# A selective scan with 16 states a channel: products with C taken four groups at a time, and loads of decays moved forward in the queue

## The reference, cut to what matters

```
u, z = split(h @ in_proj_w);  u = silu(conv(u))
dt_r, Bm, Cm = split(u @ x_proj_w);  dt = softplus(dt_r @ dt_proj_w + dt_proj_b)
A = -exp(A_log)
for t in range(512):
    hst = exp(dt[t] * A) * hst + dt[t] * B[t] * u[t]     # 256 x 16 states
    y[t] = sum over the 16 states of hst * C[t]
y = (y + u * D) * silu(z);  return y @ out_proj_w
```

## Time and profile before

| | us |
|---|---|
| median of 3 runs | 1230.9 (1224.32 to 1238.44) |
| profiled execution | 1228.28 |
| its span, first to last instruction | 1226.5 |
| VectorE busy in the span | 938.6 (77%) |
| TensorE busy | 871.2 (71%) |
| GpSimd busy | 701.0 (57%) |
| ScalarE busy | 505.5 (41%) |
| first product with B of batch 1, last of batch 8 | 482.3, 1202.4 |

### The profile page before, as it was taken

The page is one execution under the profiler, slowest core; times in us unless marked ns, Lnnn a source line. Parts: engine busy times, 40 slices in busy tenths (PEclk is TensorE's granted clock), DMA queues, the critical chain, the costliest instruction groups (busy, mean ns, idle before and its releaser), DMA issues. The chain is left out here.

```text
span 1226.5 us, 12808 instructions
## 1 busy us (share of the span) xinstructions
PE 871.2 (71%) x3620; PEld 412.1 (34%) x3620; DVE 938.6 (77%) x1280; ACT 505.5 (41%) x840; POOL 701.0 (57%) x427
## 2 busy tenths in 40 slices
PE   3668988888888656676587687688777688664552
PEld 0123333333333323344244344344434344311120
DVE  3467787977977445799469879688979779899973
ACT  0112212123123322473376386385495485663230
POOL 1021122031113561379569877569989879789996
PEclk9568788788897867699689899797999889875575
DMA  4886746666450352767766766767877767646631
GB/s 127 208 180 144 187 140 153 184 171 152 118 142 14 99 155 63 155 145 165 185 196 176 188 207 167 158 215 172 207 217 169 182 207 174 206 141 126 163 86 28
DMA packets 102849, 192.30 MB, mean 157 GB/s; under 512 B 13147, under 2 KB 68124, under 8 KB 90364
## 3 DMA queue, kind: packets, MB, share of 16 engines
q1 hardware_dynamic: 91516, 183.07, 57.2%
q0 software_dynamic: 11264, 8.43, 4.2%
HBM read 146.80 MB, written 32.06 MB: 146 GB/s over the span
## 5 line engine op out<-in xcount | busy, mean ns | idle before, releaser
L1681 POOL TENSOR_TENSOR hs<-hs,c_rep 128x1024 f32<-128x1024 f32 x128 | 332.0, 2604 | 87.7 <-DVE hs L1931 86.9
L1922 DVE TENSOR_TENSOR p_s_du<-p_s_du,b_rep 128x512 f32<-128x512 f32 x256 | 175.4, 685 | 49.5 <-PE p_s_du L2029 46.2
L2029 PE MATMUL p_s_du<-block_in,spread 96*128 96x512 bf16 x256 | 112.9, 442 | 115.5 <-DVE hs L1931 109.0
L1931 DVE TENSOR_TENSOR_SCAN hs<-decays,p_s_du 128x512 f32<-128x512 f32 x132 | 161.1, 1221 | 13.5 <-DVE p_s_du L1922 0.5
L1931 DVE TENSOR_TENSOR_SCAN hs<-slots,p_s_du 128x512 f32<-128x512 f32 x100 | 122.1, 1221 | 19.7 <-ACT slots L1826 9.7
L802 DVE TENSOR_TENSOR value_prod<-p_eb_y_acc,v 128x512 f32<-128x512 f32 x128 | 83.9, 685 | 56.6 <-PE p_eb_y_acc L1109 47.1
L513 POOL TENSOR_TENSOR sc<-ex,ex_part 128x1024 f32<-128x1024 f32 x8 | 17.0, 2129 | 171.6 <-ACT ex_part L619 171.6
L1826 ACT ACTIVATE decays<-decays,a_neg 128x512 f32<-128x512 f32 x132 | 91.7, 718 | 49.4 <-DMA decays<-dt_rows 39.3
L1720 POOL DMA_INDIRECT y_xr<-moe_sums,position x64 | 105.4, 1647 | 10.8 <-issue 8.2
L1686 POOL TENSOR_TENSOR y_hid<-y_hid,g_in 128x512 f32<-128x512 f32 x64 | 99.0, 1548 | 20.3 <-DVE y_hid L1944 19.8
L2029 PEld LDWEIGHTS p_s_du<-block_in,spread 96*128 96x128 bf16 x256 | 26.1, 102 | 249.4 <-DVE hs L1931 179.0
(11 more groups left out here) (193 smaller groups left out, 1751.6 us busy)
## 6 DMA issues: line engine op xcount, KB each, us to landing
decays<-dt_rows SPq DMA_DIRECT2D x33, 1024.0 KB
qb<-rq_rows SPq DMA_DIRECT2D x32, 1024.0 KB, 13.5
slots<-dt_rows SPq DMA_DIRECT2D x25, 1024.0 KB
wm<-in_wmoe SPq DMA_DIRECT2D x48, 384.0 KB
moe_rows<-zeros SPq DMA_DIRECT2D x8, 774.0 KB, 6.0
xg<-moe_rows SPq DMA_DIRECT2D x48, 129.0 KB
stack<-ex_part SPq DMA_DIRECT2D x96, 64.0 KB
block_in<-y_part SPq DMA_DIRECT2D x192, 32.0 KB
```

What stands on the lines that cost most here:

```text
L1681: nc.gpsimd.tensor_tensor(hs[:, n:n + 2], hs[:, n:n + 2], c_rep[p][:].unsqueeze(1).to_broadcast([128, 2, T]), ALU.mult)\
L1922: nc.vector.tensor_tensor(p_du[:, k % 2], p_du[:, k % 2], b_rep[p][:], ALU.mult).then_inc(dbu_done.sem, 1)
L1931: nc.vector.tensor_tensor_scan(hs[:, n % NA], home(8 * (b - 1) + k // 4)[:, bass.ts(j, T)], p_du[:, k % 2], 0.0, ALU.mult, ALU.add).then_i ...
L2029: nc.tensor.matmul(p_du[:, k % 2], spread[:, i], block_in[:, (2 * b + s) % NB, j], start=True, stop=True).then_inc(du_full.sem, 1)
```

## The change

- `times_c` takes four groups an instruction and waits for all four scans; it is called at k = 4, 8, ... 28 and at k = 0 of the next batch, where it was called at every even k. `gather_y` waits for one such instruction instead of two. On GpSimd the experts' `hidden` and `steps` come ahead of it within a k.
- `load_decays` comes first among a group's issues, ahead of weights and rows, and at other k: 0, 4, 8, 12, 16 for quads 3 to 7 (before: 2, 6, ... 18), and 22, 24, 28 for quads 0 to 2 of the next batch (before: 22, 26, 30). Weights come ahead of rows.
- Later: the skip of the second half by one group (4 to 5), its gate (5 to 6), its projection (9 to 13), the result (11 to 15), silu (5 to 6), the copies of B and C (16 to 19), the stores of the tiles by two groups.
- Earlier by one group: `log_in`, `softplus_cut`, `softplus_end`, `steps`.

```diff
--- before.py
+++ after.py
@@ -1400,7 +1400,7 @@
     da_done = count("da_done", GROUPS)
     dbu_done = count("dbu_done", GROUPS)
     scanned = count("scanned", GROUPS)
-    hc_done = count("hc_done", GROUPS // 2)
+    hc_done = count("hc_done", GROUPS // 4)
     gathered = count("gathered", GROUPS // 4)
     y1_done = count("y1_done", ST)
     y_done = count("y_done", ST)
@@ -1443,7 +1443,7 @@
                     plan.append((dict(rows=begin_at - 8 + 2 * h, weights=begin_at - 6 + 2 * h, turn=begin_at + h, gate=begin_at + 2 + h,
                                       hidden=then + 2 if h else begin_at + 6, up=then if h else begin_at + 4,
                                       half=then + 1 if h else begin_at + 5, down=then + 5 if h else then + 1,
-                                      weigh=then + 6 if h else then + 2, store=then + 8 if h else then + 4),
+                                      weigh=then + 6 if h else then + 2, store=then + 10 if h else then + 6),
                                  b, h, tile, len(plan) + 1))
     tile_unit = {tile: v for _, _, _, tile, v in plan if tile is not None}
 
@@ -1608,20 +1608,20 @@
                     tail(k)
                     if k == 23:
                         load_xr(0)
+                if b == 1 and k in (4, 8, 12, 15, 18):
+                    load_decays(1, {4: 3, 8: 4, 12: 5, 15: 6, 18: 7}[k])
+                if 1 < b <= B and k % 4 == 0 and k < 20:
+                    load_decays(b, (k + 12) // 4)
+                if nxt and k in (22, 24, 28):
+                    load_decays(b + 1, (k - 20) // 4)
+                for _, _, j, _ in due(b, k, "weights"):
+                    if j is not None:
+                        load_weights(j)
                 for _, _, j, _ in due(b, k, "rows"):
                     if j is not None:
                         load_rows(j)
-                for _, _, j, _ in due(b, k, "weights"):
-                    if j is not None:
-                        load_weights(j)
-                if b == 1 and k in (4, 8, 12, 15, 18):
-                    load_decays(1, {4: 3, 8: 4, 12: 5, 15: 6, 18: 7}[k])
-                if 1 < b <= B and k % 4 == 2 and k < 20:
-                    load_decays(b, (k + 10) // 4)
                 if b == 4 and k == 30:
                     load_xr(1)
-                if nxt and k % 4 == 2 and k > 20:
-                    load_decays(b + 1, (k - 22) // 4)
                 for _, _, j, _ in due(b, k, "store"):
                     if j is not None:
                         store_tile(j)
@@ -1633,7 +1633,7 @@
                 if nxt:
                     if k == 10:
                         store_bc(b + 1)
-                    if k == 16:
+                    if k == 19:
                         repeat_bc(b + 1, 1 - p)
                     if k in (19, 21):
                         store_dt(b + 1, (k - 19) // 2)
@@ -1674,11 +1674,11 @@
 
         def times_c(b, p, i):
 
-            pool.wait_ge(scanned.sem, scanned.at(b, 2 * i + 2))
+            pool.wait_ge(scanned.sem, scanned.at(b, 4 * i + 4))
             if i == 0:
                 pool.wait_ge(bc_in.sem, bc_in.at(b))
-            n = (GROUPS * (b - 1) + 2 * i) % NA
-            nc.gpsimd.tensor_tensor(hs[:, n:n + 2], hs[:, n:n + 2], c_rep[p][:].unsqueeze(1).to_broadcast([128, 2, T]), ALU.mult)\
+            n = (GROUPS * (b - 1) + 4 * i) % NA
+            nc.gpsimd.tensor_tensor(hs[:, n:n + 4], hs[:, n:n + 4], c_rep[p][:].unsqueeze(1).to_broadcast([128, 4, T]), ALU.mult)\
                 .then_inc(hc_done.sem, 1)
 
         def hidden(v):
@@ -1729,18 +1729,18 @@
                 turn = GROUPS * (b - 1) + k - 14
                 if 0 <= turn < 4 * GT and turn % 2 == 0:
                     send(*divmod(turn // 2, GT))
-                if old and k == 0:
-                    times_c(b - 1, q, GROUPS // 2 - 1)
-                if new and k and k % 2 == 0:
-                    times_c(b, p, k // 2 - 1)
+                if nxt and k in (17, 19):
+                    steps(b + 1, q, (k - 17) // 2)
                 for _, _, j, v in due(b, k, "hidden"):
                     hidden(v)
-                if old and k == 5:
+                if old and k == 0:
+                    times_c(b - 1, q, GROUPS // 4 - 1)
+                if new and k and k % 4 == 0:
+                    times_c(b, p, k // 4 - 1)
+                if old and k == 6:
                     gate_y(b - 1, q, 1)
                 if new and k == 21:
                     gate_y(b, p, 0)
-                if nxt and k in (18, 20):
-                    steps(b + 1, q, (k - 18) // 2)
                 if (b, k) in bring:
                     fetch(*bring[b, k])
 
@@ -1869,7 +1869,7 @@
                         gated(b + 2, (k - 26) // 3)
                 if not nxt:
                     continue
-                if k == 5:
+                if k == 6:
                     silu_u(b + 1, q)
                     silu_z(b + 1, q)
                 if k == 9:
@@ -1880,7 +1880,6 @@
                     exp_z(b + 1)
                 if k == 14:
                     one_more(b + 1)
-                if k == 15:
                     log_in(b + 1)
                 if k in (20, 23):
                     first_part(b + 1, (k - 20) // 3)
@@ -1962,17 +1961,17 @@
                     tail(k)
                 for _, _, j, v in due(b, k, "half"):
                     half(v)
-                if old and k == 4:
+                if old and k == 5:
                     skip(b - 1, q, 1)
-                if old and k == 11:
+                if old and k == (15 if nxt else 11):
                     result(b - 1)
                 if new and k == 20:
                     skip(b, p, 0)
                 if not nxt:
                     continue
+                if k == 15:
+                    softplus_cut(b + 1)
                 if k == 16:
-                    softplus_cut(b + 1)
-                if k == 17:
                     softplus_end(b + 1)
                 if k in (21, 24):
                     second_rest(b + 1, (k - 21) // 3)
@@ -2030,7 +2029,7 @@
 
         def gather_y(b, q):
 
-            pe.wait_ge(hc_done.sem, hc_done.at(b, 2 * q + 2))
+            pe.wait_ge(hc_done.sem, hc_done.at(b, q + 1))
             if q % 4 == 0:
                 pe.wait_ge(y1_done.sem, y1_done.at(b, q // 4) if q else y1_done.at(b - 1))
             for k in range(4 * q, 4 * q + 4):
@@ -2132,7 +2131,7 @@
                         gather_y(b, (k - 7) // 4)
                 if old and k == 3:
                     gather_y(b - 1, GROUPS // 4 - 1)
-                if old and k == 9:
+                if old and k == (13 if nxt else 9):
                     out_proj(b - 1, 1)
                 if new and k == 24:
                     out_proj(b, 0)
```

## The result

| | before | after |
|---|---|---|
| median on the same chip, 4 runs each | 1232.87 us | 1269.54 us (1266.94 to 1271.09) |
| ratio, 95% interval | | 1.0302 [1.0236, 1.0367] |
| span of the profiled execution | 1226.5 | 1265.1 |
| first product with B of batch 1 to the span's end | 744.2 | 783.4 |

The whole difference lies in the second layer (39.2 us of its time, 38.6 of the span). The forecast was 1206 us.

What follows compares the result with a forecast made beforehand. Waits and stretched instructions on VectorE were taken to lift a batch from 77 to 91 us. Terms -18 - 10 - 9.5 + 16 - 2.5 = -24 took 1228.3 to 1204, forecast 1206 us with the median's offset; range 1176 to 1243.

Steps and rivals of the forecast that it cites:

- Loads of decays, -18: VectorE's scans waiting for ScalarE's exponentials: earlier loads and later silu remove 18 of 22.7 us.
- the skip, -10: VectorE's skip products waiting for TensorE's sums over states, moved from group 4 to 5: 10 of 11.8 us go.
- Batch starts and group 11, -9.5: Products with B waiting for TensorE: 5 of 22 us go at batch starts, 4.5 of 9 at group 11.
- a rival (+49, chance 0.13): Batch starts: pieces of dt*u land behind a megabyte more, 7 us at each of seven starts, 1255 us; chance 0.13.
- The sentence on the weights: Weights stand behind a decay load at three places a batch; if late, TensorE waits, as with batch 2's 10.4 us.
- The lock, +16: VectorE's instructions with two SBUF inputs wait out longer GpSimd ones: softplus's end +18, splitting 2 better; bounds -10 to +70.
- The splitting: VectorE's splitting of dt*u, groups 21 to 26: loss of 36 us in all, as before, at 2.6 + 2.5 a batch.
- The end, -2.5: From the middle of batch 7 to the end, where GpSimd is the bound, some 12 merged instructions save 2.5 us.
- The cover named in part (3): TensorE's sum over a quad comes 5.7 us later, against 4.55; without that 1.2, up to 2 us a quad, batches 5, 6.
- The null case: Loads leave hardly sooner, or gains at groups 4 and 9 are waited for at the next start: 1228 us; chance 0.22.
- what was to show it: Right: no wait over 1 us before scans at groups 8-10 or group 5's skip; softplus 3 to 4, products 4.5 to 4.6.
- the signs of being wrong: `block_in` releasing 5 us or more at every start; TensorE waiting for `hs` before batch 7; weights releasing an expert's gate.

Runs made afterwards that it cites:

- Experiment 8: The changed kernel with SyncE's order and products with C as before, leaving only the moved steps: ratio 1.0000 to the kernel before.
- M alone: Only the moved steps (skip, silu, softplus, projection, result, stores and others), with loads and products with C as in the kernel before: ratio 1.0000 to it.
- L alone: The kernel before with only the change's places of loads, rows and weights in SyncE's order: ratio 1.0372 to the kernel before.
- the halved kernels: Decay loads halved from batch 3 in the changed kernel, in it with two-group products with C, and in the kernel before: 0.9893, 0.9833, 0.9657 of the kernel before.
- Experiment 5: The changed kernel with each four-group product with C made as two back-to-back instructions of two groups: ratio 1.0287 to the kernel before.

## Why the prediction was wrong

**Loads of decays, -18, and the skip, -10: right as waits, wrong as time.** The scans' waits fell by 22 us and the skip's by 10. Experiment 8 shows that this was worth nothing by itself: the moved steps took both away and the time stayed. The sentence that failed is "Both lie on VectorE's own queue, so they count in full; what is late next is TensorE's queue, already counted below". It was not counted.

For the skip the trace of the kernel before shows why. In batch 4, TensorE's turning of an expert's rows, which stands ahead of the sum over states, waited both for ScalarE's copy, held behind a load of decays as the prediction says, and for the rows themselves:

```profile
790.02 0.29 PEld L2048 LDWEIGHTS p_a_g<-ident,xg 128*128 128x128 f32 x2 [4.25 <-DMA xg<-moe_rows]
```

```profile
790.05 0.66 PE L2048 MATMUL p_a_g<-ident,xg 128*128 128x128 f32 x2 [3.99 <-ACT xgt L1832]
```

The two came within 0.4 us of each other in each of batches 2 to 6. With ScalarE alone sooner, the rows still hold TensorE there, and the skip's wait turns up one group later: with M alone the skip's 12 us went to none and groups 3 to 6 from none to 11. In the changed kernel what TensorE needed of ScalarE there had come 6 to 9 us before the rows in these batches.

**Batch starts and group 11, -9.5: the step that failed.** Group 11 did come free (groups 7 to 14 together went from 14 to 10 us). But the starts rose from 22 to 31 us, and groups 3 to 6 from nothing to 30 (some 11 of which are the skip's old wait, as M alone shows), for which there was no term: together +35 instead of -9.5. The text had named the pieces as a rival (+49, chance 0.13) and had the right mechanism there: small transfers behind a megabyte more. Its 7 us a start is what L alone shows (53.6 in seven). What spoke against it in the text, that quad 0 is issued 5 us sooner and has landed when quad 1 is queued, did not come about: in batch 4 quad 0 was issued 3 us sooner (counted from the start of batch 3), and in batches 2 to 8 quad 1 was queued 6.0 to 12.2 us before quad 0 had landed. Still, with the moved steps the starts wait 31 to 41 us instead of 60. And the sentence on the weights ("if they land late, TensorE waits") belonged to the rows: the change put them behind both the load and the weights, and TensorE waits for them ahead of group 5's product (30.0 us in six waits, 19.1 in seven before).

**The lock, +16: right in kind, half in size.** It cost 32 us (40 to 72). The two instructions of softplus took 39.1 us instead of 19.1, +20 where the sum had +18, but the end alone +13, and +7 came from the first, which had no term; and the length of a quad was right (4.55 us estimated, 4.53 median). The splitting was put at the same loss as before (36), with the one at group 21 unchanged: it lost 51.4 + 17.9 - 19.0 = 50 instead of 38. The instruction of line 1910 (`conv<-dtu,y_part`) averages 3.67 us instead of 2.09, and loses 21 us at group 21 (11 before) as well as 21 at group 24 (8 before). At group 21 of batch 4 a quad starts one microsecond ahead of it (GpSimd, VectorE):

```profile
853.61 4.50 POOL L1681 TENSOR_TENSOR hs<-hs,c_rep 128x2048 f32<-128x2048 f32 x1
```

```profile
854.62 4.04 DVE L1910 TENSOR_TENSOR conv<-dtu,y_part 128x512 f32<-128x512 f32 x1
```

That is the rule of the Trainium skill, "SBUF — State Buffer", section "Who interferes with whom", and the trace agrees with it in the rows shown: VectorE's instruction ends 0.5 to 1.1 us behind GpSimd's. What the sum got wrong is where the quads start, not that VectorE waits for their end.

**The end, -2.5: wrong sign.** From the first product with B of batch 8 to its last scan 77.7 us instead of 71.7. The cover named in part (3), 1.2 us between a quad's product and the sum over it, went here and not in batches 5 and 6: up to the last scan, TensorE's weight loads for the sums over states wait 27.6 us for GpSimd's products, all of it in batches 7 and 8, against 9.7 before.

With these sizes the terms come to -22 - 10 + 35 + 32 + 6 = 41 us, against 39 measured in the layer.

**The null case's reason** was the best one in the text ("each load has slack somewhere else"; "what is gained at groups 4 and 9 is waited for at the next start"), only its size was not. With 73 and 77% of the DMA engines' time taken in batches 4 and 5 a megabyte earlier is a megabyte ahead of something else.

Of what was to show it: no waits before scans at groups 8 to 10 or before the skip, quads of 4.5 us and softplus stretched to 3.6 us came as forecast; the signs of being wrong came in part: `block_in` released a wait of TensorE at each start, of 1.0 to 8.7 us, TensorE waited for GpSimd's products from batch 7 on and not before, and rows, not weights, held the expert's work.

What stays open: why the waits of the halved kernels are still 37 to 40 us (11 to 15 of them stand at the start of batch 2, whose loads are whole), and how much of the change's 39 us is due to L's own places of rows and weights rather than to the loads.

## What to carry to other kernels

Before moving a large load forward, ask which small transfers are in flight at that time and who waits for them. In this kernel, with DMA at three quarters of its time, every order tried left 73 us of waits or more, and only fewer bytes brought them down to 40. Before merging GpSimd instructions, list the VectorE instructions with two SBUF inputs: each can wait for the whole merged one. And a wait is worth its length only if the next resource is ahead by that much: look at every semaphore that the waiting instruction needs, and not only at the one that came last. A run in which the wait is taken away by other means (experiment 8) tells it cheaply.

## What the hardware showed that I had not expected

**A queue of its own carries a small transfer only a little past large ones.** 32 KB pieces on ScalarE's queue, with the megabyte loads on SyncE's, landed 11.3 to 15.3 us after their last issue (7.0 in batch 8), on the same queue 14.4 to 18.2 us; beside 512 KB loads on the same queue 4.1 to 7.3 us. The Trainium skill, "DMA: Bandwidth & Descriptors", section "Issuing engines are not separate DMA queues", has SyncE and ScalarE share the same 16 engines; the trace agrees, in that the megabytes on one queue still held the pieces on the other. Its section "Queues, rings and completion order" says that an engine changes between the queues packet by packet; what such a turn costs each of the twelve pieces no run here shows.

**An instruction of VectorE can be passed by two of GpSimd.** In batch 7 of the changed kernel (GpSimd and VectorE, group 22):

```profile
1136.14 1.87 POOL L1686 TENSOR_TENSOR y_hid<-y_hid,g_in 128x512 f32<-128x512 f32 x1
1136.30 6.73 DVE L1915 TENSOR_TENSOR y_part<-conv,y_part 128x512 bf16<-128x512 f32 x1
...
1137.37 5.10 POOL L1681 TENSOR_TENSOR hs<-hs,c_rep 128x2048 f32<-128x2048 f32 x1
```

VectorE's instruction, 0.68 us alone, started behind an expert's product on GpSimd, and was not let in between that and the quad: it ended 0.6 us behind the quad, at 1143.03. (GpSimd's spans are rough; the two overlap in the record.) Here two instructions back to back held VectorE as long as both. Experiment 5 has both cases: VectorE was passed by three in the lines shown, and got in between two elsewhere, as at group 16 of batch 4, where the end of softplus took 1.46 us.
